# Deformable sampling: corner sums kept in four SBUF tiles, and a fourth PSUM bank in place of the accumulator

## The reference, cut to what matters

```python
samp = corner(y0, x0, (1 - wy1) * (1 - wx1)) + corner(y0, x0 + 1, (1 - wy1) * wx1) \
     + corner(y0 + 1, x0, wy1 * (1 - wx1)) + corner(y0 + 1, x0 + 1, wy1 * wx1)
samp = samp * mask[:, None]                                   # [b, c, tap, h, w]
out = jnp.einsum('bckhw,ock->bohw', samp, dcn_w.reshape(COUT, C, KK))   # 9 taps
```

## Time and profile before

| | |
|---|---|
| time, median of 3 runs | 6881.6 us (6878.8 to 6883.12) |
| span of the profiled execution | 7648.3 us |
| ahead of the first gather | 3838 us |
| sampling, first gather to last | 3711 us |
| behind the last gather | about 100 us |
| DVE, PE, POOL, ACT busy while sampling | 2257, 2103, 2212, 1300 us of 3711 |

### The profile page before, as it was taken

The page is one execution under the profiler, slowest core; times in us unless marked ns, Lnnn a source line. Parts: engine busy times, 40 slices in busy tenths (PEclk is TensorE's granted clock), DMA queues, the critical chain, the costliest instruction groups (busy, mean ns, idle before and its releaser), DMA issues. The chain is left out here.

```text
span 7648.3 us, 89071 instructions
## 1 busy us (share of the span) xinstructions
PE 5717.8 (75%) x21147; PEld 3269.1 (43%) x21147; DVE 5490.3 (72%) x12779; ACT 3409.0 (45%) x7221; POOL 4111.0 (54%) x3871
## 2 busy tenths in 40 slices
PE   5999999999989999999865565655656565565442
PEld 2444444444478888888532222322223232232111
DVE  6999999999967777778565666556566665665556
ACT  4888888888855211111233333333333333333333
POOL 4999999999910001000055555655556565565663
PEclk9999999999999999999987676877778777687665
DMA  5445444444420000000156555555555665555567
GB/s 193 170 179 180 167 169 172 170 168 167 168 87 3 3 0 23 0 0 0 42 164 198 164 184 178 168 183 168 180 180 172 193 184 183 178 176 179 178 182 265
DMA packets 306397, 1093.60 MB, mean 143 GB/s; under 512 B 56560, under 2 KB 58639, under 8 KB 264604
## 3 DMA queue, kind: packets, MB, share of 16 engines
q0 software_dynamic: 187440, 625.23, 27.1%
q1 hardware_dynamic: 118516, 464.08, 17.0%
HBM read 997.72 MB, written 91.37 MB: 142 GB/s over the span
## 5 line engine op out<-in xcount | busy, mean ns | idle before, releaser
L1281 POOL DMA_INDIRECT d_ring<-corner_table,d_idx_now x2304 | 2212.2, 960 | 1635.9 <-issue 950.2
L1481 PE MATMUL d_ps_s<-small,d_mix 128*128 128x128 f32 x2304 | 489.6, 350 | 1544.2 <-DVE d_mix L1653 1010.5
L979 POOL TENSOR_TENSOR X<-X 128x512 f32<-128x512 f32 x1024 | 1289.7, 1277 | 168.3 <-DVE X L1017 150.9
L1481 PEld LDWEIGHTS d_ps_s<-small,d_mix 128*128 128x128 f32 x2304 | 327.8, 176 | 2071.0 <-issue 1089.5
L1653 DVE SCALAR_TENSOR_TENSOR d_acc<-d_ring,d_w_now,d_mix 128x128 f32<-128x128 f32 x2304 | 660.9, 354 | 694.3 <-ACT d_mix L1327 321.5
L1017 DVE TENSOR_TENSOR_SCAN X<-X,m_pB 128x512 f32<-128x512 f32 x896 | 1132.4, 1269 | 0.0
L873 PE MATMUL m_pY<-X,small 128*128 128x512 f32 x2048 | 1040.4, 605 | 90.3 <-POOL X L979 90.2
L277 PE MATMUL prop_ps<-prop_parts,prop_w_hi 128*128 128x480 f32 (+4 forms) x4536 | 1099.8, 387 | 4.6 <-DVE prop_parts L286 4.6
L1327 ACT ACTIVATE d_mix<-d_ring,d_w_now 128x128 f32<-128x128 f32 x2304 | 732.3, 390 | 719.1 <-DMA d_ring<-corner_table,d_idx_now 659.1
L277 PEld LDWEIGHTS prop_ps<-prop_parts,prop_w_hi 128*128 128x128 f32 x4536 | 816.0, 188 | 133.4 <-DVE prop_parts L286 5.4
L1411 PE MATMUL d_ps_out<-d_samp,d_dcn_w 128*128 128x512 f32 x1152 | 832.0, 815 | 7.9 <-ACT X L1314 5.8
(11 more groups left out here) (231 smaller groups left out, 7744.8 us busy)
## 6 DMA issues: line engine op xcount, KB each, us to landing
X<-c_scratch SPq DMA_DIRECT2D x256, 1024.0 KB, 4.9
d_ring<-corner_table,d_idx_now POOLq DMA_INDIRECT x2304
corner_table<-d_tT SPq DMA_DIRECT2D x120, 256.0 KB
X<-in_x SPq DMA_DIRECT2D x8, 2048.0 KB, 15.2
m_res<-in_x SPq DMA_DIRECT2D x64, 256.0 KB, 4.6
x_scratch<-m_res SPq DMA_DIRECT2D x64, 256.0 KB, 2.1
x_scratch<-X SPq DMA_DIRECT2D x8, 2048.0 KB
b_x<-x_scratch POOLq DMA_DIRECT2D x16, 1024.0 KB, 11.7
```

The costliest lines, as they stand in the source:

```text
L979: pool.tensor_tensor(hc[:, n % NHC, :], h[:, n, :], Cb[:, n, :], ALU.mult).then_inc(s.HC, 1)
L1281: pool.indirect_dma_start(out=ring[:, m % RING, :], out_offset=None, in_=flat, in_offset=bass.IndirectOffsetOnAxis(ap=idx_now[:, c % 2, m: ...
L1481: turned = pe.transpose(ps_s[k % 3][:, t, :], R[:, k % 3, t, :], G.ident)
```

## The change

The corner sums stay in `R`: all three corners read `ring` and `R` and write `R`, in place. `acc` goes, and its PSUM bank becomes a fourth `ps_s`. `R` has four tiles in place of three (2 KB more of each partition). `R` and `ps_s` are chosen by `slot(c, k)`. DVE's wait for the whole of its own tap before (for `acc`) goes. ACT may write corner 0 four taps behind the transposes in place of three. `BEHIND` is 3, so `keep_samples`, the contraction, `keep_output` and `statistics` move one tap back. `DEEP`, `ring`, `samp` (three tiles) and the gathers stay.

```diff
-    BEHIND = 2
+    BEHIND = 3
+    MIXES = 4
...
-            R = sb2("d_mix", [P, 3, NT, P])
+            R = sb2("d_mix", [P, MIXES, NT, P])
...
-            acc = bank("d_acc", [P, NT, P])
-            ps_s = [bank(f"d_ps_s{i}", [P, NT, P]) for i in range(3)]
+            ps_s = [bank(f"d_ps_s{i}", [P, NT, P]) for i in range(MIXES)]
...
+            def slot(c, k):
+                return (TAPS * c + k) % MIXES
...
-                    def keep_samples(gG, k):
+                    def keep_samples(gG, c, k):
                         after(act, s_turn, TAPS * gG + k)
                         after(act, s_dcn, TAPS * gG + k, 3)
-                        act.activation(samp[:, k % 3, :], ps_s[k % 3][:].rearrange("p t c -> p (t c)"),
+                        act.activation(samp[:, k % 3, :], ps_s[slot(c, k)][:].rearrange("p t c -> p (t c)"),
                                        ACT.Copy).then_inc(s_samp, 1)
...
-                        after(act, s_turn, TAPS * gG + k, 3)
+                        after(act, s_turn, TAPS * gG + k, MIXES)
                         for t in range(NT):
                             m = NT * k + t
-                            r0 = act.activation(R[:, k % 3, t, :], ring[:, m % RING, 0:P], ACT.Copy,
+                            r0 = act.activation(R[:, slot(c, k), t, :], ring[:, m % RING, 0:P], ACT.Copy,
                                                 scale=w_now[:, c % 2, 4 * m:4 * m + 1])
...
-                        pe.wait_ge(s_samp, TAPS * gG + (k - 3 + 1 + CREDIT))
+                        pe.wait_ge(s_samp, TAPS * gG + (k - MIXES + 1 + CREDIT))
                         after(pe, s_mix, TAPS * gG + k)
                         for t in range(NT):
-                            turned = pe.transpose(ps_s[k % 3][:, t, :], R[:, k % 3, t, :], G.ident)
+                            turned = pe.transpose(ps_s[slot(c, k)][:, t, :], R[:, slot(c, k), t, :], G.ident)
...
-                        after(dve, s_mix, TAPS * gG + k, 1)
                         dve.wait_ge(s_r0, TAPS * gG + (k + 1))
                         first = NT * (TAPS * c + k)
                         for corner in range(1, 4):
...
                                 mixed = dve.scalar_tensor_tensor(
-                                    R[:, k % 3, t, :] if corner == 3 else acc[:, t, :],
+                                    R[:, slot(c, k), t, :],
                                     ring[:, m % RING, corner * P:(corner + 1) * P],
                                     w_now[:, c % 2, 4 * m + corner:4 * m + corner + 1],
-                                    R[:, k % 3, t, :] if corner == 1 else acc[:, t, :],
+                                    R[:, slot(c, k), t, :],
                                     ALU.mult, ALU.add)
```

More of the change, by code:

```diff
@@ L1330, in sample @@
                         if k >= BEHIND:
-                            keep_samples(gG, k - BEHIND)
+                            keep_samples(gG, c, k - BEHIND)
                         elif not (s.first and c == 0):
-                            keep_samples(gG - 1, k - BEHIND + TAPS)
+                            keep_samples(gG - 1, c + NCH - 1, k - BEHIND + TAPS)
                         if k == BEHIND and not (s.first and c == 0):
@@ L1399, in end @@
                         for k in range(TAPS - BEHIND, TAPS):
-                            keep_samples(B * NCH - 1, k)
+                            keep_samples(B * NCH - 1, NCH - 1, k)
                         keep_output(B * NCH - 1)
```

## The result

| | median | runs |
|---|---|---|
| before | 6882.08 us | 6878.8 to 6883.12, 4 runs |
| change | 7195.74 us | 7179.21 to 7203.24, 4 runs |

The change is slower: ratio 1.0453, interval 1.0438 to 1.0468, or 314 us more. I had forecast 6930 (+0.7%) with a range up to 6960. The sign is right and the size is not; the loss is more than six times the forecast.

The account below looks back on a forecast made before the run. The prediction took POOL's issuing of gathers to bound the timed sampling. It summed 6881.6 + 47 (gathers held up by in-place sums) + 0 (coupling) + 2 (the end) = 6930.6, said 6930 us (+0.7%), range 6858 to 6960.

Parts of the forecast that it names:

- POOL as the bound: Sampling: 2304 gathers at 1.26 us take POOL 2903 us, leaving it at most some 41 us of waits when timed.
- The missing 767 us: Profiled span 7648.3 us exceeds the timed median by 766.7; claimed to be sampling waits made by the profiled execution.
- Corner sums in place: Corners 2 and 3 get two SBUF inputs: 1014 gather starts at 46 ns each cost POOL 47 us (29 to 64).
- the likeliest case: Gathers held up by the corner sums with two SBUF inputs: 6930 us, own range 6908 to 6948, chance 0.57.
- Rival 2: Twelve two-input instructions in a row leave POOL no free window for 3.1 us: 91 us, 6975 us, chance 0.07.
- DVE's own time: Corner additions without PSUM: at most 80 ns more per tap, 3.98 us for 3.9, hidden under POOL's 5.04.
- rival 5: DVE gets quicker without PSUM, 0.20 for 0.26 us per instruction, fewer collisions: 34 us, 6918 us, chance 0.05.
- The coupling: Four tiles, four banks, contraction three taps behind, in the sampling: taken as 0 (down to -41 us).
- rival 4: The looser coupling wins, as timed runs have more than 41 us of waits: 6866 or 6826 us, chance 0.16.
- DVE's wait for its own tap: DVE's wait for its own last tap goes; two groups wait 26.4 and 25.9 us; under POOL's pace worth 0.
- The end: Behind the last transposes stand 8 contraction matmuls in place of 6 (5.31 us): +1.8 us.
- Rival 3: Longer gathers only shorten POOL's waits for mixed taps, so no change: 6882 us, chance 0.15.

Follow-up runs that it names:

- fresh profile of before: The unchanged kernel profiled a second time, on a chip where it takes 6882 us: 6884.22 us profiled, 6882.79 not.
- in place only: Against the kernel before: corner sums in place in R, no accumulator, but three R, three banks, BEHIND = 2. 7294.65 us, ratio 1.0592.
- two pauses: The changed kernel, but DVE waits at the first instruction of corners 2 and 3 for the whole corner ahead. 6957.1 us, ratio 1.0110 to before.
- rows of six: The changed kernel with a single gap behind the sixth of each tap's twelve instructions. 6933.01 us, 1.0076 to before; on the slow chip 7618.61, 1.0025.
- corners 1 and 3: Kernel before, but corner 3 added in place and corner 2 moved from PSUM to SBUF. 7095.53 us, ratio 1.0312; on the slow chip 7563.53, 0.9936.
- corner 0 in PSUM: Against before: ACT writes corner 0 to one of two PSUM accumulators, no two-SBUF-input corner addition, two ps_s banks. 6866.20 us, 0.9978; slow chip 7632.21, 1.0028.
- corners 1 and 2: Kernel before, but corner 1 added in place in R and corner 2 moved from R to the accumulator. 7591.35 us where before takes 7622.70, ratio 0.9973.
- Coupling only: The change with acc, its wait and three banks put back; four R and BEHIND = 3 stay. 6884.05 us, ratio 1.0005 to before.
- the earlier trace: The first profile of the kernel before, the one the prediction read: span 7648.3 us; its chip is not on record.
- the change, third time: The changed kernel run on a chip where the kernel before takes 7622.70 us: 7599.28 us, ratio 0.9987.

## Why the prediction was right in direction and wrong in size

**POOL as the bound: right.** I had 2903 us of POOL's own time and 41 us of waits in a timed run; the fresh profile of before shows 2902 and 43. The timed differences on those chips follow the gathers' busy time: +334 us and +319 in the two profiled executions of after and before; +431 and +412 in place only, +64 and +74 with two pauses, +34 and +51 for rows of six, +228 and +214 for corners 1 and 3, -20 and -15 with corner 0 in PSUM.

**The missing 767 us: right in effect, wrong in cause.** I said that the waits were "nearly all of the profiled execution's making". Profiling makes none that can be seen; what the runs leave is the chip.

**"Corner sums in place": the term that failed.** "1014 x 46 ns = 47 us" has the right pair of instructions, about the right number of starts (950) and the wrong price: they cost 321 us, 338 ns each. The places 1 to 6 of a row bear out the 46 (32 to 65 ns, no start held). From place 7 on the price is another: 312 us for 604 starts, 517 ns each. The price came from corner 1 in the kernel before, which stands in places 1 to 4 because DVE nearly always waits ahead of it (568 us for ACT in the fresh profile). The low end of the likeliest case's range, 6908, was a slip besides: 6882 + 2 + 29 is 6913.

**Rival 2 named the mechanism and I gave it 0.07 and 91 us.** It said that twelve in a row "leave POOL no free window". My argument against it, "corner 1's four instructions are back to back too", is the step of reasoning that fails: four in a row hold a gather for some 0.17 us at most in the fresh profile of before (one odd case 0.23), twelve for over 1 us. "Corners 1 and 3" against "corners 1 and 2" shows it, and the two pauses take most of it away.

**DVE's own time: right.** The twelve stand 0.263 us apart with both inputs in SBUF, where corners 1 and 2 showed 0.26. So rival 5 fell. The Trainium skill (Perfetto Trace Analysis, "Optimizing Scalar/DVE Operations") gives DVE more access overhead on PSUM than on SBUF; these start-to-start times show no gain from leaving PSUM.

**The coupling: right at 0.** Coupling only is at 1.0005, and rival 4 fell. ACT's copy (L1308) had no wait in the sampling of the fresh profile of before, so there was nothing to save. DVE's wait for its own tap (26 us in the earlier trace rows) was no loss either, and without it rows run over two taps: 44 taps follow the one before without a gap in "the change, third time" and 6 in after, none in either profile of before.

**The end.** I added 1.8 us for two more matmuls. They are there, eight in 4.90 us, but the six of the earlier trace rows took 5.31, so it can't be seen.

**Rival 3, absorbed:** wrong where before takes 6882, right where it takes 7623.

**What I said the profile would show.** Median 949 (952), greatest DVE duration over 400 ns (418) and the issue gap of 0.30 came true; the gather's mean was to be 975 and is 1104, and L1653's mean 354 and is 344. ACT's waits ahead of its copy were to be well below 160 us and are 4.9, but before has as few on this kind of chip.

**The page that spoke against the change.** Of the corner additions only those with two SBUF inputs make a gather longer, in every run here: with none of them, in "corner 0 in PSUM, again", starts in all twelve places cost at most 2 ns on average. That agrees with the Trainium skill (SBUF — State Buffer, "Who interferes with whom"). Its inference that descriptor generation is not held up is contradicted by the 396 gathers that were held over 0.22 us in places 8 to 12 of after.

## What to carry to other kernels

Where GpSimd's indirect DMAs set the pace, look at what VectorE does in the moment each one starts. Keep one input of its long rows in PSUM, or break a row of two-input instructions within six by a wait; two pauses of 0.15 us in each tap were worth 239 us or more here. A price read from short rows must not be used for long ones, so look at what keeps them short before you take a wait out. Before a profile's waits are explained, see that it comes from a chip on which the kernel takes its timed median.

## What the runs showed of the hardware that I had not expected

- A gather that starts in instruction 1 to 6 of a back-to-back row of corner additions is let in after at most some 0.18 us, if nothing follows on the row. From 8 on (sometimes from 7) it waits until the row's last two-input instruction is nearly done: 1.15 us at place 8, 0.4 at place 11. Single-input additions ahead in the tap count too; behind `statistics` or the copies the count does not hold as it stands. That this is a matter of who is served first at a shared read path is only argued; the runs show the pattern, not its inside.
- One program has two times on different chips, 6882 and about 7610 us, with the same instructions. The same edit is 1.0312 on one and 0.9936 on the other ("corners 1 and 3"). The slower kind is where POOL waits 602 us for mixed taps, against 77 on the other. Why its taps come late stays open, and so does why "corners 1 and 3" is faster there with its gathers longer, and "corner 0 in PSUM" slower with its gathers shorter.
- A copy can make a gather longer too, though it has one input: in "corner 0 in PSUM, again" the gathers at 5392.71 and 6220.29 us start as DVE copies indices and weights within SBUF (L1636 and L1637, 0.18 and 0.23 us), with nothing of DVE's behind for 0.9 us or more, and take 1.08 and 1.05 us.
